# x1 rows that carry the position of the edge that wrote them, and a second recurrent pass that gathers by it

## The reference

```python
h = max(layernorm(x), 0); x = x + L0(h)     # attention, softmax over edges of one dst, tanh
h = max(layernorm(x), 0); x = x + L1(h)     # GATv2 attention, batch norm over nodes, gelu
h = max(layernorm(x), 0); x = x + L2(h)     # attention grouped by src, 18 edge attributes
h = max(layernorm(x), 0); x = x + L3(h)     # two recurrent passes, then batch norm

# L3
output, hstate = h, zeros
for _ in range(2):
    t = einsum('nd,rde->rne', output, weight)        # three relation types
    msg = t[rel_type, src] * norm[:, None]
    swh = segment_sum(msg, dst, num_segments=N_NODES)
    hstate = gru_cell(swh, hstate, ...)              # sigmoid gates, tanh candidate
    output = hstate
```

## Time and profile before

| what | us |
|---|---|
| median of 3 runs | 8856.25 (8849.47 to 8865.16) |
| the profiled execution | 8784.2 |
| its span, first to last instruction | 8782.3 |
| busy: POOL, DVE, PE, ACT | 5878.3, 5410.8, 4269.5, 2377.9 |

### The profile page before, as it was taken

How to read it: one execution, slowest core, us unless ns; L and a number is a source line. 1 busy time by engine, 2 the same in 40 slices (tenths; PEclk the granted TensorE clock), 3 DMA queues, 4 the chain that set the end, 5 groups by cost and what they waited for, 6 DMA issues and landing times. The chain is left out here.

```text
span 8782.3 us, 75502 instructions
## 1 busy us (share of the span) xinstructions
PE 4269.5 (49%) x11974; PEld 2124.2 (24%) x11974; DVE 5410.8 (62%) x9130; ACT 2377.9 (27%) x4661; POOL 5878.3 (67%) x6277
## 2 busy tenths in 40 slices
PE   0002444443666666200266666665666666767740
PEld 0001111111222222000134434443333333333320
DVE  6854777775777777797166666665333335555554
ACT  1112333333333333332133333332111112222210
POOL 5875666665566665687677777775666666666665
PEclk9999999999666666555555555555666667777765
DMA  2332222222333333575111111111111121111149
GB/s 81 102 96 83 80 83 80 83 84 80 91 95 90 91 94 91 152 212 157 19 41 42 41 42 42 42 42 39 52 52 52 52 52 40 41 41 41 41 110 263
DMA packets 873137, 682.12 MB, mean 78 GB/s; under 512 B 663969, under 2 KB 697566, under 8 KB 872879
## 3 DMA queue, kind: packets, MB, share of 16 engines
q1 hardware_dynamic: 705463, 488.34, 19.6%
q0 software_dynamic: 163104, 167.63, 8.2%
q10 hardware_dynamic: 4512, 25.60, 1.0%
HBM read 385.09 MB, written 312.41 MB: 79 GB/s over the span
## 5 line engine op out<-in xcount | busy, mean ns | idle before, releaser
L728 POOL DMA_INDIRECT l_rows<-x,l_num x1176 | 1186.4, 1009 | 460.4 <-issue 373.0
L753 POOL DMA_INDIRECT o<-l_out,l_snum x392 | 407.8, 1040 | 391.4 <-DVEq L1228 284.2
L1330 POOL DMA_INDIRECT er_edge_rows<-eat,all_perm x392 | 531.6, 1356 | 145.0 <-issue 134.1
L753 POOL DMA_INDIRECT x<-l_out,l_snum x392 | 414.9, 1059 | 303.0 <-DVEq L1082 197.0
L728 POOL DMA_INDIRECT l_rows<-in_x,l_num x392 | 444.6, 1134 | 169.5 <-issue 158.2
L753 POOL DMA_INDIRECT xh<-l_out,l_snum x392 | 395.1, 1008 | 223.4 <-issue 165.4
L753 POOL DMA_INDIRECT g<-l3a_out,l3a_snum x392 | 402.2, 1026 | 200.8 <-issue 170.7
L753 POOL DMA_INDIRECT g<-l3b_out,l3b_snum x392 | 399.5, 1019 | 204.1 <-issue 177.4
L728 POOL DMA_INDIRECT l3b_rows<-g,l3b_num x392 | 388.7, 992 | 170.0 <-issue 102.7
L728 POOL DMA_INDIRECT l3a_rows<-xh,l3a_num x392 | 379.5, 968 | 169.6 <-issue 159.1
L936 POOL DMA_INDIRECT pre_src_rows<-in_x,all_idx_src x392 | 388.3, 991 | 140.8 <-issue 126.0
(11 more groups left out here) (366 smaller groups left out, 12763.4 us busy)
## 6 DMA issues: line engine op xcount, KB each, us to landing
l_far<-far_d SPq DMA_DIRECT2D x196, 256.0 KB
g<-l_fill SPq DMA_DIRECT2D x194, 256.0 KB
l_far<-far_s SPq DMA_DIRECT2D x98, 256.0 KB
o<-l_fill_o SPq DMA_DIRECT2D x97, 256.0 KB
xh<-l_fill_h SPq DMA_DIRECT2D x97, 256.0 KB
ts_xin<-in_x SPq DMA_DIRECT2D x31, 800.0 KB
x<-ts_row SPq DMA_DIRECT2D x31, 800.0 KB
d_xin<-x SPq DMA_DIRECT2D x31, 800.0 KB, 4.5
```

Source lines behind the costliest of these rows:

```text
L728: pool.indirect_dma_start(self.buf[k.u][:, j, at:at + w], None, table, bass.IndirectOffsetOnAxis(ap=self.num[k.u][:, m, j:j + 1], axis=0)) ...
L753: pool.indirect_dma_start(self.table, bass.IndirectOffsetOnAxis(ap=self.num[k.u][:, j:j + 1], axis=0), self.out[k.u][:, j, 0:self.cols], N ...
L1330: pool.indirect_dma_start(c.edge_rows[:, t, :], None, eat, bass.IndirectOffsetOnAxis(ap=c.perm[:, t:t + 1], axis=0)).then_inc(c.edges_gath ...
```

## The change

Each row of `x1` becomes 65 words: one word ahead of the 64 features holds the edge position whose result the row is, or 98 × 512 = 50176 where no edge wrote it. `tables_start` fills that word with the constant; in `conv_gat` ACT copies the positions of a chunk (`c.pos`, an iota) ahead of the features of the rows to be scattered. `conv_gatv2` gathers 65-word rows, and ACT copies the first word of each gathered row into `c.idx_pos`, then frees the row buffer, which DVE did before. Row 50176 of `g_rows` holds the quiet row. l3a keeps its edge-ordered store and scatters nothing; l3b gathers from `g_rows` by `idx_pos`. `g1`, its fill in l0 and that scatter are gone. In both `conv_rgcn` scopes DVE now does `hm` of `k0` ahead of the scan of `k1`, and PE the transposes of `k0` ahead of the gates of `k1`.

```diff
+POS = 1
@@ tables_start
-    s.row = [s.sb(f"row{u}", [NP, NR, D]) for u in range(2)]
+    s.row = [s.sb(f"row{u}", [NP, NR, POS + D]) for u in range(2)]
+        for u in range(2):
+            pool.memset(s.row[u][:, :, 0:POS].bitcast(I32), c.NCH * CE).then_inc(s.no_pos, 1)
+        pool.iota(c.pos[:], pattern=[[P, c.NT]], base=0, channel_multiplier=1).then_inc(s.no_pos, 1)
+        pool.wait_ge(s.no_pos, 3)
-            pool.tensor_tensor(s.row[k.u][:], s.xin[k.u][:], over_rows(s.tb[0:NP, :], NR),
+            pool.tensor_tensor(s.row[k.u][:, :, POS:POS + D], s.xin[k.u][:], over_rows(s.tb[0:NP, :], NR),
@@ conv_gat
-        sct = Scatter(s, tab1, D, c.scat_d, c.N)
+        sct = Scatter(s, tab1, POS + D, c.scat_d, c.N)
-                        fill.store(sp, k)
+                        sct.free(act, k2)
+                        act.activation(sct.out[k2.u][:, :, 0:POS].bitcast(I32), c.pos[:, bass.ds(k2.i * TPC, TPC)].unsqueeze(2),
+                                       ACT.Copy).then_inc(m["pos_put"], 1)
@@ conv_gatv2
-        rows = Rows(s, [(x1, D, 0, c.idx_src)], 2 * D)
+        rows = Rows(s, [(x1, POS + D, 0, c.idx_src)], 2 * (POS + D))
                         norm.square(act, k0.n)
+                        act.activation(c.idx_pos[:, bass.ds(k0.i * TPC, TPC)].unsqueeze(2), rows.buf[k0.u][:, :, 0:POS].bitcast(I32),
+                                       ACT.Copy).then_inc(m["pos_kept"], 1)
+                        act.wait_ge(m["pos_kept"], k0.n)
+                        act.sem_inc(rows.rows_free, 1)
-                        dve.sem_inc(rows.rows_free, 1)
@@ nodes_second
-        xin = [s.sb(f"xin{u}", [NP, NR, D]) for u in range(2)]
+        xrow = [s.sb(f"xrow{u}", [NP, NR, POS + D]) for u in range(2)]
+        xin = [r[:, :, POS:POS + D] for r in xrow]
@@ conv_rgcn
-        rows = Rows(s, [(table, width, 0, c.idx_src)], width)
-        sct = Scatter(s, out_table, D, c.scat_d, c.N)
+        rows = Rows(s, [(table, width, 0, c.idx_pos if k_ else c.idx_src)], width)
+        sct = Scatter(s, out_table, D, c.scat_d, c.N) if k_ else Kept(s, D)
+                if k_ == 0:
+                    sp.dma_start(g_rows[c.NCH * CE:c.NCH * CE + 1, :], c.quiet[0][0:1, :]).then_inc(quiet_stored, 16)
-                gather_scatter(pool, c, rows, sct, 3)
+                gather_scatter(pool, c, rows, sct if k_ else None, 3)
@@ gnn
-        conv_rgcn(nc, c, "l3a", dram, xh, 0, g_rows, g1)
-        conv_rgcn(nc, c, "l3b", dram, g1, 1, g_rows, g2)
+        conv_rgcn(nc, c, "l3a", dram, xh, 0, g_rows, None)
+        conv_rgcn(nc, c, "l3b", dram, g_rows, 1, g_rows, g2)
```

More of the change, by code:

```diff
@@ L763, in done, with __init__ @@
             eng.wait_ge(self.scattered[u], 16 * TPC * turns)
+class Kept:
+    def __init__(self, s, width):
+        self.out = [s.sb(f"out{u}", [P, TPC, width]) for u in range(2)]
+        self.out_ready = s.sem("out_ready")
 def gather_scatter(pool, c, rows, sct, lag):
@@ L999, in body @@
                         sp.wait_ge(sct.out_ready, old.n)
-                        sp.dma_start(edge_rows(e1, old), sct.out[old.u][:]).then_inc(e_stored[old.u], 16)
+                        sp.dma_start(edge_rows(e1, old), sct.out[old.u][:, :, POS:POS + D]).then_inc(e_stored[old.u], 16)
                 slots(sp, c.NCH, 2, body)
-                fill.done(sp, c)
                 fill_o.done(sp, c)
@@ L1080, in body @@
                         dve.wait_ge(m["tanh_ready"], k2.n)
-                        step(dve.scalar_tensor_tensor(sct.out[k2.u][:], r2[:], -2.0, x_one[k2.u][:], ALU.mult, ALU.add))
+                        step(dve.scalar_tensor_tensor(sct.out[k2.u][:, :, POS:POS + D], r2[:], -2.0, x_one[k2.u][:], ALU.mult, ALU.add))
+                        dve.wait_ge(m["pos_put"], k2.n)
                         dve.sem_inc(sct.out_ready, 1)
@@ L1114, in conv_gatv2 @@
     with Scope(nc, "l1") as s:
-        rows = Rows(s, [(x1, D, 0, c.idx_src)], 2 * D)
+        rows = Rows(s, [(x1, POS + D, 0, c.idx_src)], 2 * (POS + D))
+        pairs = [b[:].rearrange("p j (a f) -> p (j a) f", a=2)[:, :, POS:POS + D] for b in rows.buf]
         sct = Scatter(s, o1, 2 * D, c.scat_d, c.N, D)
@@ L1220, in body @@
                         dve.wait_ge(dst_loaded[k0.u], 16 * (k0.t + 1))
-                        norm.center(dve, step, two(rows.buf[k0.u][:]))
-                        dve.sem_inc(rows.rows_free, 1)
+                        norm.center(dve, step, pairs[k0.u])
                     if k2:
@@ L1344, in body @@
                             dve.wait_ge(stored[old.u], 32 * old.t)
-                        step(dve.tensor_tensor(out[old.u][:], y[old.u][:], xin[old.u][:], ALU.add))
+                        step(dve.tensor_tensor(out[old.u][:], y[old.u][:], xin[old.u], ALU.add))
                         dve.sem_inc(m["x2_done"], 1)
@@ L1724, in body @@
                         dve.sem_inc(rows.rows_free, 1)
+                    if k1:
+                        dve.wait_ge(keep_loaded[k1.u], 16 * (k1.t + 1))
+                        dve.wait_ge(m["msg_done"], k1.n)
+                        step(dve.tensor_tensor_scan(acc[k1.u][0:D, :], keep[k1.u][:], p_msg[:],
+                                                    0.0 if k1.start else acc[1 - k1.u][0:D, CE - 1:CE], ALU.mult, ALU.add))
+                        dve.sem_inc(m["acc_ready"], 1)
                     if k2:
-                        sct.free(dve, k2)
-                        if k_ == 0 and not k2.first:
+                        if k_:
+                            sct.free(dve, k2)
+                        elif not k2.first:
                             dve.wait_ge(g_stored[k2.u], 16 * k2.t)
@@ L1759, in body @@
                 def body(k0, k1, k2):
+                    if k0:
+                        hold(pe, m["hm_ready"], k0.n)
+                        for j in range(TPC):
+                            cols = slice(j * P, (j + 1) * P)
+                            pe.transpose(p_01[:, cols], hm[:, j, 0:P], c.ident[:])
+                            ins = pe.transpose(p_2[:, cols], pair[:, j, :], c.ident[:])
+                        ins.then_inc(m["turned"], 1)
                     if k1:
@@ L1768, in body @@
                     if k0:
-                        hold(pe, m["hm_ready"], k0.n)
-                        for j in range(TPC):
-                            cols = slice(j * P, (j + 1) * P)
-                            pe.transpose(p_01[:, cols], hm[:, j, 0:P], c.ident[:])
-                            ins = pe.transpose(p_2[:, cols], pair[:, j, :], c.ident[:])
-                        ins.then_inc(m["turned"], 1)
                         hold(pe, m["h_out"], k0.n)
```

37 lines of the change are left out of this document (16 added, 21 removed).

## The result

The changed kernel takes 8527.57 us (median of 4 runs, 8491.67 to 8534.98) against 8855.58 us (4 runs, 8849.47 to 8865.16) on the same chip: ratio 0.9621, 95% interval 0.9592 to 0.9649, 328 us less. The forecast was 384 us less. The profiled execution took 8527.84 us, with a span of 8526.1 us.

The account below looks back on a forecast made before the run. POOL's indirect DMAs were taken to bound l3a; dropping its scatters gains 374 us plus some 10 at its end, together 384, all else 0, so 8856 − 384 = 8472 us, range 8395 to 8660 us.

Parts of the forecast that it names:

- POOL was the bound of l3a and the scatters carry the sum: l3a: POOL sets the 12.01 us step; without scatters it falls to 8.15 us, gaining 374 us.
- tail: End of l3a, behind the last products: the three scatters left there go, some 10 us.
- The ring at either level of the clock: l3a's next bound: DVE-PE-ACT dependence loop, 7.7 us per chunk at high clock; PE itself, 9.9 at low.
- 80% of the chunks at the high clock: l3a: 0.8 × 7.7 + 0.2 × 9.9 = 8.15 us per chunk.
- a rival, that without waits for DMAs the clock stays high: l3a: every chunk takes 7.7 us, 428 us gained, 8428 us in all; chance 17%.
- The new order: `conv_rgcn` scopes: l3a's loop stands on DVE in just the new sequence, 7.7 us per chunk at high clock.
- l3b 0: l3b: still eight indirect DMAs per chunk, so POOL's 12.1 us stay; 0, range −10 to +20 us.
- the repeated row: l3b: gathers often hit row 50176; taken as 0; rival: slower gathers, up to 576 us, 9048 us, chance 3%.
- Loads and ACT's copies 0: Loads of x1 in d2 grow 1.6%, ACT copies in l0 and l1 are hidden in idle time; both 0.
- l1 0: l1: ACT's copy is hidden and freeing rows about 1 us later delays nothing; 0.
- a bound for the first stage: First stage: POOL's adds into unaligned 65-word rows cost at most 49 us, taken as 0.
- 72 us from the profiled execution to the median: Whole kernel: the median lies 72 us above the profiled execution; the same was added to 8400 us, giving 8472.

Follow-up runs that it names:

- scatter_kept: The changed kernel, but l3a still scatters, into a table of its own that nobody reads: 8748.06 us, ratio 1.0022 to the kernel before.
- order_only: The kernel before with only the new order of DVE and PE work in both `conv_rgcn` scopes: 8763.99 us, ratio 1.001.
- more_matmuls: The changed kernel with eight idle 128-column matmuls on PE behind each chunk's messages in l3a: 8334.56 us, ratio 0.9507 to the kernel before.
- old_order: The changed kernel with the order of the kernel before in both `conv_rgcn` scopes: 8435.85 us, ratio 0.9642 to the kernel before.
- one_row: The changed kernel with all gathers of l3b reading the quiet row 50176: 8387.49 us, ratio 0.9579 to the kernel before.
- sets 1 to 3: The three sets of follow-up runs, each compared within itself; the kernel before took 8754.3, 8755.0 and 8782.3 us in them.
- before_again: The kernel before, unchanged, in one more profiled run: 8757.34 us.

## Why the prediction was right, step by step

- *POOL was the bound of l3a and the scatters carry the sum*: shown. scatter_kept puts them back and has the old step; order_only alone gains nothing. Products plus tail gave 349 us of 384. With dl's 30 and l3b's 7 us lost and 15 gained ahead of l2 that makes 328: what I had at 0 or had not named moved both ways and partly cancelled.
- *The ring at either level of the clock*: 7.7 us at the high one, where more_matmuls measured 7.59 at a clock of 0.99.
- *80% of the chunks at the high clock*: this is the mis-sized term. The mean clock is 0.80, which is 60% of the time at the high level, and 0.6 × 7.7 + 0.4 × 9.9 = 8.6 us, near the measured 8.49. The holes came out about as I wrote (1.94 us the longest in the two steps shown); the inference from them, that so short a hole leaves the clock high in four chunks of five, was wrong. The step gave 97 × (12.01 − 8.49) = 341 us instead of 374, the tail 8 instead of 10. Of the section "HAM oscillation" of TensorE: Matmul & The Clock Gate (the Trainium skill), the first half, that bursts parted by waits fall back, agrees with the rows of before (the low level behind a hole of 2.50 us, 0.66 over the stage). What I drew from it as a rival, that without waits for DMAs the clock stays high, does not hold here: DVE waits 7 us for rows in the whole stage and the clock is 0.80.
- *The new order*: I worked the ring out for it and took for granted that it mattered. old_order shows it to be worth 23 us: its ring is about as long, and that the omission cost the forecast nothing is luck.
- *l3b 0*: 6.8 us longer in the profile, inside the range. Its cause is not settled. The new order alone makes l3b 10 us longer (order_only), and the change of the table with the old order makes it 11 us longer (old_order, 1225.8 us), so the two do not add up. It is not the repeated row: with that row alone l3b is the shortest of all, 1211.6 us (one_row), and the row costs only DMA time that nobody waits for.
- *Loads and ACT's copies 0*: right in l0 (1407.8 to 1407.0 us) and in the first stage: POOL's adds into rows of 65 words took 3565 ns in the middle, 3563 before.

```profile
L944 POOL TENSOR_TENSOR ts_row<-ts_xin,ts_tb x32: 3558/3565/3861, 65.4 to 705.6; 128x1600 f32<-128x1600 f32 x32
```

- *l1 0*: it was 14.5 us shorter (1461.7 to 1447.2). I had asked what ACT's new work costs, and not what DVE is spared.
- *dl not named at all*: 29.8 us back, the largest omission. Nothing in it was edited; its start moved, and of the three lengths that the pass has in the traces it came out in the longest. The rows showed that it could: the earlier trace rows have POOL's add at 5108 ns in dl and 3574 in the first stage, and I used the pair only as a bound for the first stage.
- *72 us from the profiled execution to the median*: the changed kernel's median did come out that much later, and its trace shows it as a longer l2. But I put the 72 us on top without knowing what they were, so that this part held is luck. In sets 1 to 3 no l2 was longer than 1796.5 us, and before_again was within 3 us of its median. The cause stays open.

## What to carry to other kernels

When the bound engine is relieved, write down the ring that comes next and time it at both levels of PE's clock; then ask whether a piece of it can be done a turn earlier, which here was worth 236 us, ten times the order on the engines. A level of the clock that is only argued from the length of PE's holes is a guess: here it was the term that missed. Two engines that add in the same pass over large tiles should be put on one if it has the time: the pass took 263 us with all adds on DVE and 283 to 324 us with one on POOL. And a stage that no edit touches can move by tens of us (l2, dl), so the stages are to be compared one by one before an overall difference is explained.

## What the runs showed of the hardware

- A DVE addition of two 128x1600 tiles that starts just behind a POOL addition waits for all of it: 5.16 us instead of 1.83, ending 1.7 us after the other's end; POOL's takes 3.55 us alone and 5.12 us when DVE's is ahead. The Trainium skill says so (SBUF — State Buffer, section "SBUF: two separate sides": whichever starts first holds the shared ports for its whole instruction), and the trace agrees.
- More matmuls made the kernel faster: eight idle ones per chunk raised the clock of the stage from 0.80 to 0.99, its step fell from 8.49 to 7.59 us, and the kernel by 84 us.
- Reads of one row by all descriptors more than doubled the busy share of the DMA engines (0.20 to 0.46) at the same 40 GB/s.
- Rows of 260 bytes were written, gathered and scattered at no cost that these runs can show: POOL's adds 3565 against 3563 ns, the gathers of l1 981 against 985 ns, l0 1407.0 against 1407.8 us.
